# A Mamba-style layer with a mixture of experts: its scan in sub-chunks of 64 tokens instead of chunks of 128

## The reference, cut to what matters

```python
x = input_tensor @ Wx.T; z = input_tensor @ Wz.T
x = silu(causal_conv(x, conv_w, conv_b))             # 2 sequences of 4096 tokens, 512 channels
b = (x @ Wb.T).reshape(bsz, seq, 8, 64); c = (x @ Wc.T).reshape(bsz, seq, 8, 64)
dt = softplus(x @ Wdt.T + b_dt); a = -exp(log_a)
# for every token t and each of the 8 heads:
state = exp(dt_t * a) * state + (dt_t * b_t)[:, None] * x_t[None, :]      # 64 x 64
y_t   = c_t @ state
y = y + d_param * x; out = (groupnorm(y) * silu(z)) @ Wout.T
# beside it: router, top-k tokens of each of 8 experts, up and down projections, scatter-add
```

## Time and profile before

| | |
|---|---|
| median of 3 runs | 1219.45 us (1218.78 to 1220.4) |
| profiled execution, span from first to last instruction | 1219.8 us |
| TensorE busy, weight loads busy | 1203.0 us (99%), 993.8 us (81%) |
| VectorE, ScalarE, GpSimd busy | 951.8, 714.7, 791.4 us |
| 16 DMA queues, mean busy share over the span | q1 47.5%, q0 8.2% |
| scan, from the first turned x to the last `state_parts` | 191.1 us to 771.3 us |

### The profile page before, as it was taken

The page is one execution under the profiler, slowest core; times in us unless marked ns, Lnnn a source line. Parts: engine busy times, 40 slices in busy tenths (PEclk is TensorE's granted clock), DMA queues, the critical chain, the costliest instruction groups (busy, mean ns, idle before and its releaser), DMA issues.

```text
span 1219.8 us, 30709 instructions
## 1 busy us (share of the span) xinstructions
PE 1203.0 (99%) x11883; PEld 993.8 (81%) x11883; DVE 951.8 (78%) x2027; ACT 714.7 (59%) x1465; POOL 791.4 (65%) x788
## 2 busy tenths in 40 slices
PE   8999999999999999999999999999999999999998
PEld 4666668888888888888888887788888888899998
DVE  7999977898985777777778767987768775777676
ACT  6999985555565465555555556555455443555444
POOL 4889945545555577677776758367666655576773
PEclk9999999999999999999999999999999999999999
DMA  9799764643343443443343435564544446799995
GB/s 300 252 343 341 289 242 140 114 136 120 134 140 117 136 126 122 141 129 119 134 135 122 136 124 169 175 156 92 111 91 92 98 87 127 261 324 321 332 332 167
DMA packets 112351, 214.28 MB, mean 176 GB/s; under 512 B 20432, under 2 KB 78544, under 8 KB 107600
## 3 DMA queue, kind: packets, MB, share of 16 engines
q1 hardware_dynamic: 99056, 195.04, 47.5%
q0 software_dynamic: 12288, 17.05, 8.2%
q10 hardware_dynamic: 864, 0.24, 0.1%
HBM read 131.03 MB, written 81.26 MB: 174 GB/s over the span
## 4 chain that ended last, share of the span: by engine, by line
PE 86%; DVE 5%; DMA 3%; SPq 2%; ACT 2%; issue 1%; POOL 1%; ACTq 0%; DVEq 0%; POOLq 0%
PE ps L1439 27%; PE ps L1801 10%; PE ps L2311 8%; PE ps L2290 7%; PE ps L2075 6%; PE ps L1520 4%; PE ps L1487 3%; PE ps L2077 3%; PE ps L1546 3%; PE ps L1509 3%; PE ps L1531 2%; PE ps L1560 2%; PE ps L690 1%; PE ps L743 1%; DMA parts_dram<-xn_lo 1%
## 5 line engine op out<-in xcount | busy, mean ns | idle before, releaser
L1395 ACT ACTIVATE decay<-tap,ncum 128x128 f32<-128x128 f32 x344 | 105.7, 392 | 141.4 <-POOL tap L1289 141.4
L1985 POOL DMA_INDIRECT ffn_dram<-ob,idx x64 | 108.4, 1694 | 85.8 <-DVE ob L1904 74.6
L1296 POOL TENSOR_TENSOR x_lo<-x,x_hi 128x512 fp32r<-128x512 f32 x56 | 77.3, 1380 | 104.3 <-ACT x_hi L1368 104.3
L1174 DVE TENSOR_TENSOR x_dt<-ps,dt 128x512 f32<-128x512 f32 x64 | 44.3, 691 | 120.3 <-PE ps L1546 120.3
L2075 PE MATMUL ps<-dn,mid_hi 128*128 128x512 f32 x288 | 104.9, 399 | 0.5 <-DVE moments L1875 0.5
L2033 ACT ACTIVATE mid<-ps,b_up 128x512 f32<-128x512 f32 x96 | 65.9, 690 | 67.2 <-PE ps L1801 56.3
L1439 PE MATMUL ps<-x_hi,w_hi_b 128*128 128x512 f32 x240 | 99.4, 414 | 0.0
L1439 PE MATMUL ps<-x_hi,w_hi_c 128*128 128x512 f32 x240 | 99.3, 414 | 0.0
L2166 POOL TENSOR_SCALAR yc<-yc,gn_scale,gn_shift 128x512 f32<-128x512 f32 x56 | 76.5, 1378 | 33.0 <-DMA yc<-y_dram 32.9
L1439 PE MATMUL ps<-x_lo,w_hi_b 128*128 128x512 f32 x240 | 94.4, 393 | 0.0
L1439 PE MATMUL ps<-x_lo,w_hi_c 128*128 128x512 f32 x240 | 94.2, 393 | 0.0
(11 more groups left out here) (318 smaller groups left out, 3962.2 us busy)
## 6 DMA issues: line engine op xcount, KB each, us to landing
tap<-cum_dram SPq DMA_DIRECT2D x43, 512.0 KB
x_dram<-x SPq DMA_DIRECT2D x16, 1024.0 KB, 5.3
yc<-y_dram SPq DMA_DIRECT2D x16, 1024.0 KB, 6.9
y_dram<-yb SPq DMA_DIRECT2D x30, 512.0 KB, 2.8
x<-x_dram SPq DMA_DIRECT2D x26, 512.0 KB, 3.9
cum_row<-cum_dram SPq DMA_DIRECT2D x21, 512.0 KB
rows_dram<-xn SPq DMA_DIRECT2D x16, 512.0 KB, 3.3
ffn_dram<-zero SPq DMA_DIRECT2D x64, 128.0 KB
```

Of the source, the lines that this page charges most:

```text
L1296: nc.gpsimd.tensor_tensor(low, raw, high, ALU.subtract).then_inc(x_lo_ready, 1)
L1395: n = nc.scalar.activation(decay[g % 2][:, h, :], cum_row[g % NR][:, row, :], ACT.Exp, bias=t.ncum[:, g, h:h + 1])
L1985: pool.indirect_dma_start(out=t.ffn_dram, out_offset=bass.IndirectOffsetOnAxis(ap=t.idx[:, e, h * HC + c:h * HC + c + 1], axis=0), in_=ob[ ...
```

## The change

The unit of the recurrence becomes 64 tokens: cum starts anew at each half of a chunk, the triangle of a head is now two diagonal 64x64 blocks, and what the later half needs of the earlier one comes through a state in the middle of the chunk (`state_mid`). There are thus two state steps a chunk. All products are 64x64x64: `update` fills, for each token half p, its own bank (`ps_g[p]`, beside the scores), `state_parts` is run twice a chunk, once with the state at its start and once with `state_mid`. The exchange of halves and its copies go away. The work of chunk g+1 is prepared a chunk earlier: TensorE turns x and B of g+1 in chunk g, turned B is made between the projections, but behind the C projection in the last chunk of a block, and `update(g+1)` follows `scores(g+1)`. SP loads four pieces of rows a chunk in place of one (the sums within halves for keys, and the heads of a partition's half for queries; together again 512 KB).

```diff
-    c[:, C_TRI:C_TRI + P] = i[:, None] <= i[None, :]
-    c[:, C_ONES:C_ONES + P] = 1
+    together = i[:, None] // 64 == i[None, :] // 64
+    c[:, C_TRI:C_TRI + P] = together & (i[:, None] <= i[None, :])
+    c[:, C_LATER:C_LATER + P] = together & (i[:, None] > i[None, :])
...
             pe.matmul(ps_t[0][:, 0:NT * H], t.tri, flat, start=True, stop=True).then_inc(ten, 1)
-            pe.matmul(ps_t[1][:, 0:NT * H], t.ones, flat, start=True, stop=True).then_inc(ten, 1)
+            pe.matmul(ps_t[1][:, 0:NT * H], t.later, flat, start=True, stop=True).then_inc(ten, 1)
+            for j in range(2):
+                for a in range(2):
+                    mm = pe.matmul(ps_dt[a * s.HD:(a + 1) * s.HD, j * NT * MT:(j + 1) * NT * MT],
+                                   t.headavg[:, j * s.HD:(j + 1) * s.HD], dta[:, :, a * MT:(a + 1) * MT],
+                                   start=True, stop=True, skip_group_check=True)
...
+        def shrink(g, j):
+            source = (states[g % 2], state_mid)[j]
+            n_scaled[0] += 1
+            dve.wait_ge(state_ready, ends(g)) if j == 0 else dve.wait_ge(mid_ready, g + 1)
+            v.tensor_tensor(state_tmp, source, dec[j][:, g, :].unsqueeze(2).to_broadcast([P, MT, HD]),
+                            ALU.mult).then_inc(scaled, 1)
...
+                v.tensor_tensor(state_mid, ps_new[0], state_tmp, ALU.add).then_inc(mid_ready, 1)
...
+            v.tensor_tensor(states[(g + 1) % 2], ps_new[1], state_tmp, ALU.add).then_inc(state_ready, 1)
...
         def chunk(g):
...
+            if g:
+                add_state_banks(g - 1)
+            if not first:
+                shrink(g, 0)
+            if g:
+                add_other_halves(g - 1)
...
+            if g + 1 < NT:
+                scale_x(g + 1)
+            middle_state(g)
             dve.wait_ge(exp_ready, g + 1)
-            dve.wait_ge(g_ready, g + 1)
-            for i in range(2):
-                v.tensor_tensor(mix[:, 4 * i:4 * i + 4, :],
-                                ps_g[i][:, :].rearrange("p (h n) -> p h n", h=4),
-                                decay[g % 2][:, 4 * i:4 * i + 4, :], ALU.mult).then_inc(mix_ready, 1)
...
+            if not last:
+                shrink(g, 1)
+            v.tensor_tensor(mix.rearrange("p (a h) n -> p a (h n)", a=2), ps_scores,
+                            decay[g % 2].rearrange("p (a h) n -> p a (h n)", a=2), ALU.mult).then_inc(mix_ready, 1)
+            if not last:
+                end_state(g)
             if 1 <= g <= ROUNDS:
                 next_bits(g - 1)
...
+            if g + 1 < NT:
+                weigh_b(g + 1)
...
         def update(g):
             pe.wait_ge(x_dt_ready, g + 1)
-            pe.wait_ge(b_w_ready, updates(g) + 1)
...
+            pe.wait_ge(b_w_ready, g + 1)
             for m in range(MT):
-                for a in range(2):
-                    h, i = (a * MT + m) * HD, (2 * m + a) * HD
-                    mm = pe.matmul(ps_s[a * HD:(a + 1) * HD, m * HD:(m + 1) * HD], b_w[:, i:i + HD],
-                                   x_dt[:, h:h + HD], start=(m == 0), stop=True, skip_group_check=True)
+                for p, a in ((0, 0), (1, 1), (1, 0), (0, 1)):
+                    rows, h, i = slice(p * HD, (p + 1) * HD), (a * MT + m) * HD, (2 * m + a) * HD
+                    mm = pe.matmul(ps_g[p][a * HD:(a + 1) * HD, UPD + m * HD:UPD + (m + 1) * HD],
+                                   b_w[rows, i:i + HD], x_dt[g % 2][rows, h:h + HD], start=True, stop=True,
+                                   skip_group_check=True)
...
             until(pe, y_ready, g)
...
-            pe.wait_ge(mix_ready, 2 * g + 2)
-            mm = own_parts(g)
+            pe.wait_ge(mix_ready, g + 1)
+            own_parts(g)
+            pe.wait_ge(c_dec_ready, g + 1)
             if not first:
-                until(pe, state_ready, updates(g))
-                pe.wait_ge(c_dec_ready, updates(g))
-                mm = state_parts(g)
-            mm.then_inc(y_mm, 1)
-            if g + 1 < NT:
+                pe.wait_ge(state_ready, ends(g))
+                state_parts(g, 0)
+            pe.wait_ge(mid_ready, g + 1)
+            state_parts(g, 1).then_inc(y_mm, 1)
+            if more:
                 scores(g + 1)
-            if g >= LAST and not last:
-                update(g)
+                update(g + 1)
```

More of the change, by code:

```diff
@@ L402, in do @@
                     steps[name] = done[0]
-            def do_turned(op, *parts, name):
-                do(op(*(a[:, 0] for a in parts)))
-                for r in range(2):
-                    own, other = (slice(j * s.HD, (j + 1) * s.HD) for j in (r, 1 - r))
-                    do(op(parts[0][own, 1], *(a[other, 1] for a in parts[1:])), name if r else None)
             full = [P, NT, 8]
@@ L1523, in own_parts, with state_parts @@
-            return mm
-        def state_parts(g):
+                    h, rows = 2 * q + i, slice(p * HD, (p + 1) * HD)
+                    mm = pe.matmul(ps_y[p][i * HD:(i + 1) * HD, q * P + p * HD:q * P + (p + 1) * HD],
+                                   x_dt[g % 2][rows, h * HD:(h + 1) * HD], mix[rows, h, :],
+                                   start=(q == 0), stop=False, skip_group_check=True)
+            return mm
+        def state_parts(g, j):
+            held = (states[g % 2], state_mid)[j]
@@ L1536, in _ @@
         pe.wait_ge(t.front_vec, t.front_steps["rows"])
+        turn_x(0)
+        project(1, 0, 0)
+        turn_b(0)
+        pe.wait_ge(t.tile_out, 2 * MT)
+        pe.wait_ge(t.front_sca, 6)
+        scores(0)
+        pe.wait_ge(t.front_sca, 7)
+        project(1, 0, 1, range(0, 2))
+        turn_x(1)
+        update(0)
+        project(1, 0, 1, range(2, MT))
         for g in range(NT):
             b, c = g // CH, g % CH
-            cols = slice(c * P, (c + 1) * P)
-            first, last = g % SPAN == 0, g % SPAN == SPAN - 1
@@ L1549, in _ @@
                 project(b + 1, c, 0)
-            elif c < 2:
+            elif b + 1 == NB and c < 2:
                 x.turn(pe, c)
-            else:
+            elif b + 1 == NB:
                 x.up(pe, 0, 0, range(c - 2, c - 1))
-            if g == 0:
-                pe.wait_ge(t.tile_out, 2 * MT)
-                scores(0)
-            if not last:
-                pe.wait_ge(x_dt_ready, g + 1)
-                for m in range(MT):
-                    mm = pe.transpose(ps_xb[:, m * P:(m + 1) * P], bT[b % 2][:, m, cols], t.ident)
-                mm.then_inc(b_turned, 1)
+            if more and c < CH - 1:
+                turn_b(g + 1)
```

402 lines of the change are left out of this document (184 added, 218 removed).

## The result

The changed kernel takes 1242.99 us (median of four executions, 1239.39 to 1246.57), the kernel before 1219.12 beside it. The ratio is 1.0191, 95% interval 1.0167 to 1.0215. The forecast was 1194.6 us with a range of 1184 to 1214, so it is wrong in sign. The profiled execution took 1239.39 us with a span of 1237.6; it is the fastest of the four. The median lies 3.6 us higher still, in executions whose granted clock was 0.993 to 0.995 where the profiled one had 0.997.

A forecast was written before the change was run, and what follows sets the result against it. TensorE was taken to bound 60 of 64 chunks. Savings of 1.65, 3.6, 6.6 and 14.4 us, less 0.5 and 1, gave 24.8 us off the 1219.8 span, hence a median of 1194.6 us, range 1184 to 1214.

The forecast's parts named there:

- The products on TensorE: `own_parts` to `scores`, with `update`: 1.93 us instead of 2.55; 0.55 saved a chunk, 0.45 in the lists.
- The wait of L1005: VectorE's operation lasts 1.21 us beside GpSimd's L1296; two shrinks a chunk newly open to this; outside the search 0 taken.
- Rival B: VectorE becomes the bound, meeting GpSimd's operations: search stays at 9.3, lists lose 0.2 a chunk; 1205 us, chance 0.18.
- VectorE's work: Operations gone and new on VectorE: together some 0.4 us less work a chunk.
- The search: Chunks of the bit search come out between 8.76 and 9.75 us, 9.0 taken; 3.6 us saved over chunks 4 to 15.
- VectorE's ring: In the search, from one weighting of B to the next: 8.7 us without L1005's wait, 9.75 with all of it.
- Rival A: TensorE cannot be fed at the narrow pace over 128 records, 21.6 ns each; slower, 1242 us, chance 0.11.
- The front: Before the chunks, four matmuls of 256 columns are added on TensorE: some 0.5 us lost.
- "0" for SP: SP issues four loads for one, of equal bytes, two chunks ahead: no cost.
- The last chunks: Last four chunks, without projections, where TensorE waits for `mix`: +1 us (-1 to +4).
- The sum: Whole kernel: chunks save 26.25 us, less 0.5 and 1: 24.8 us, hence 1194.6 us.

The follow-up runs named there:

- psum: The changed kernel with both shrinks' wide operand read from a PSUM bank instead of the state in SBUF: 1223.20 us, ratio 0.9997 to the kernel before.
- stt: The changed kernel with shrinks and the sums behind them replaced by eight scalar_tensor_tensor a chunk: 1224.38 us, ratio 1.0015 to the kernel before.
- stt early: The changed kernel with eight scalar_tensor_tensor for shrinks and sums, next B weighted behind the end state in three of four chunks: 1220.09 us, ratio 0.9978.

## Why the prediction was wrong

- **The products on TensorE: right.** 2.04 us for the run (1.93 forecast), chunks of 8.54 to 8.58 between the stages (8.55), 8.90 in the lists where nothing holds them (8.85).
- **The wait of L1005: the step that failed.** I had read that VectorE's operation and GpSimd's ended together, and that the two shrinks of a chunk are open to the same. Then I priced what this costs outside the search at 0 to 0.3 us a chunk and took 0, since "the idle time covers 1 us". The shrinks wait 1.01 us on average at the second place and 0.4 to 0.5 at the first; the digits, pushed into GpSimd's product, another 1.0 (1674 against 715 ns). Together 1.0 + 0.5 + 1.0 less 0.36 on the other digits, 2.1 us a chunk, use up the 23% idle, which are 2.1 us of 9.29. Taking the operand away gives back 1.9% of the time. Rival B named this mechanism, but with 0.2 us a chunk in the lists; there it was 9.67 against 8.85, 0.8. Against it I held "the lists' digits at 0.68 each"; but in the trace of before one half of them had a mean of 1161 ns and the other 715, so such a wait stood there already, in rows that the forecast did not use.
- **VectorE's work: a sum that does not add up.** "Some 0.4 us less" a chunk: its own terms, 0.6 + 0.76 + 0.2 for the sums of y less 1.36, give 0.2. The psum trace, where the shrinks do not wait, has 940.3 us of VectorE against 951.8, 0.18 a chunk, with the waits of its other operations in both. The error is small beside the waits.
- **The search: a size.** 9.0 forecast; most chunks took 9.16, and chunks 4 to 14 on average 9.35. That VectorE's ring sets it was right; with no shrinks most stayed at 9.15. The early weighting with the shrinks left the stage at 147.3 us (147.9), no shrinks with the late weighting at 146.0, and only both together reached TensorE's 8.78 and 141.4. So the place of the weighting and the waits cost together here, and neither repair was enough alone.
- **Rival A: the right question, dismissed on half an answer.** The pace of a run of 128 is as good as that of 16. What doesn't always keep up is the delivery of instructions, in blocks and not at a steady rate. The trace of before has hardly a row of it: five stops called "issue" in the scan, 2.7 us in all, four of them behind 730 us. Counting only those that end behind a packet of the instruction queue, the stops cost 6.5 to 11 us in the versions whose shrinks don't wait and whose `update` stays in the run (8.4 in stt, 9.7 in psum, 10.9 in stt early). The clock adds to this, by an estimate at most 8.5 us in stt early: half of its 17 us at 0.50.
- **The front: +3.6 instead of +0.5.** The four added matmuls, 8 records, took 1.02 us, not 0.5; another 1.0 stood there at 120 us already, ahead of them; the loads of the rows, four of 128 KB a chunk, were issued 0.6 us apart by SP where one of 512 KB took 0.32, and GpSimd's first masks waited for them. "0" for SP was wrong ahead of chunk 0 only. Not tested by an experiment.
- **The last chunks: wrong, and right only by where the line is drawn.** Chunks 60 to 62 came at +0.9, with +1 forecast. But the step from 59 to 60 took 10.19 us instead of 4.76, through the shrink of 5.37 us above, which stands in chunk 60; with it the last chunks came at +6.3, outside the -1 to +4. The mix that TensorE waits for there came late by a shrink, not by the 0.6 us of longer way that was forecast.

The sum: chunks 0 to 59 were forecast at -26.25 us and came at +14.4, the front at +3.6, the last chunks at +0.9, the rest at -1.1: +17.8, the two spans' difference. With no shrinks, the early weighting and six updates moved the span is 1207.9 and those terms are -13.5, +1.9, +0.8 and -1.1: half of the gain that was forecast. Of the other half, 9.8 us still stand in stops (between 190 and 820 us).

Left open: what decides at a boundary whether VectorE or GpSimd goes next, and why the packet with a block of instructions starts late at some boundaries and not at others. The run holds 256 of the 336 matmuls and weight loads of a lists' chunk, so about three of four boundaries fall into it; but stt early has 43 packets between 415 and 715 us and only 9 stops. The digits with an operand in PSUM weren't tried, since TensorE writes the bank that they would read.

## What to carry to other kernels

An elementwise operation that reads both operands from SBUF on VectorE must not be priced by its own duration where GpSimd works in long instructions: give it a PSUM operand, or cut GpSimd's instructions short, and count the wait through several of them. Before many short matmuls are put in one run, compare the instructions in it (here 256) with those in a packet of the instruction queue (here about 252), and look for stops called "issue" in the middle of a group; whether one is a late block can be told by a packet of that queue that landed shortly before its end (here 1.2 to 1.6 us). A stop of 2 to 3 us can cost twice, since the granted clock may fall behind it.

## What the runs showed of the hardware

- Shrinks of 128x256 with two SBUF operands: 0.41 us of work, 5.37 at worst; with one in PSUM 0.42 on average. GpSimd waits in its turn (1.20 instead of 1.04).
- A stop of TensorE for instructions ended 1.20 to 1.58 us after a packet of the instruction queue had landed, in 83 of 85 cases; the stops lasted 0.2 to 3.0 us.
- Narrow 64x64 matmuls in four quarters start every 14 to 16 ns over 128 records.
- One excursion between the 128-row layout and the quarters: 0.35 us by the timeline, 0.37 by the chunks.
- TensorE stopped 2.53 us without a fall of its clock, 2.25 us with one to 0.50 for some 3 us, and 2.98 us with one for some 6 us.
- An added 0.42 us operation on an engine in the ring of the search cost 0.3 us a chunk there, in the lists none (9.29 with and without).
